# A mixture of experts on chosen rows in tiles of slots, after a routing stage of its own

## The reference

```
x  = x + L1_ffn(layernorm(x))
scores = softmax(xf @ Wg.T)                     # 8 experts
expert_weights, expert_indices = top_k(scores, 2)
gates  = one_hot(indices) * weights / sum(weights), summed over the two
h1, h3 = xf @ W1[e].T + low rank + b1[e],  xf @ W3[e].T + low rank + b3[e]     # 128 -> 256
y_e    = (silu(h1) * h3) @ W2[e].T + low rank + b2[e]                          # 256 -> 128
y      = sum over e of gates[e] * y_e
```

## Time and profile before

| what | us |
|---|---|
| median of 3 runs | 1125.36 (1123.95 to 1134.6) |
| the profiled execution | 1127.59 |
| its span, from the first to the last instruction | 1126.4 |
| mean granted TensorE clock | 0.834 of full speed |
| PE busy | 872.6 (77%) |
| DVE busy | 773.8 (69%) |
| ACT busy | 451.6 (40%) |
| POOL busy | 426.2 (38%) |
| moved by DMA | 37.98 MB |

### The profile page before, as it was taken

The page is one execution under the profiler, slowest core; times in us unless marked ns, Lnnn a source line. Parts: engine busy times, 40 slices in busy tenths (PEclk is TensorE's granted clock), DMA queues, the critical chain, the costliest instruction groups (busy, mean ns, idle before and its releaser), DMA issues. The chain is left out here.

```text
span 1126.4 us, 20278 instructions
## 1 busy us (share of the span) xinstructions
PE 872.6 (77%) x6496; PEld 644.1 (57%) x6496; DVE 773.8 (69%) x3299; ACT 451.6 (40%) x1123; POOL 426.2 (38%) x767
## 2 busy tenths in 40 slices
PE   0976766765577998537891388988699999999998
PEld 0753433432374554424561256666488888888887
DVE  7949999999334886371130869999567666766664
ACT  1454445444103555101132657877333333333332
POOL 5213666666545542016663655655200100010000
PEclk9975666667557999767996569999799999999999
DMA  8211111111103000005533100000000000000000
GB/s 171 64 40 31 36 36 35 37 36 31 30 13 150 19 23 24 10 6 100 84 107 121 45 2 3 3 3 3 1 1 10 11 1 11 10 10 1 10 10 10
DMA packets 66078, 37.98 MB, mean 34 GB/s; under 512 B 39482, under 2 KB 60083, under 8 KB 65460
## 3 DMA queue, kind: packets, MB, share of 16 engines
q1 hardware_dynamic: 63206, 32.31, 10.5%
q0 software_dynamic: 2048, 4.20, 2.5%
q10 hardware_dynamic: 718, 0.17, 0.1%
HBM read 26.11 MB, written 10.55 MB: 33 GB/s over the span
## 5 line engine op out<-in xcount | busy, mean ns | idle before, releaser
L1759 ACT ACTIVATE e_sg<-e_ps,vec 128x512 f32<-128x512 f32 x128 | 88.1, 689 | 182.7 <-PE e_ps L1720 182.0
L1680 PEld LDWEIGHTS e_psy<-w_folded,e_hh 128*128 128x128 f32 x1024 | 124.1, 192 | 5.2
L1680 PE MATMUL e_psy<-w_folded,e_hh 128*128 128x128 f32 x1024 | 124.5, 275 | 0.0
L1858 DVE SCALAR_TENSOR_TENSOR e_hh<-e_ps,vec,e_sg 128x512 f32<-128x512 f32 x128 | 94.6, 748 | 42.5 <-ACT e_sg L1759 39.7
L1846 DVE SCALAR_TENSOR_TENSOR X<-e_psy,e_gs,X 128x128 f32<-128x128 f32 x256 | 72.1, 344 | 56.5 <-PE e_psy L1680 56.5
L1718 PE MATMUL e_ps<-e_XH,e_wh 128*128 128x512 f32 x256 | 110.0, 430 | 0.0
L1720 PE MATMUL e_ps<-e_XH,e_wl 128*128 128x512 f32 x256 | 101.7, 397 | 0.0
L1719 PE MATMUL e_ps<-e_XL,e_wh 128*128 128x512 f32 x256 | 101.4, 396 | 0.0
L1448 POOL TENSOR_SCALAR a_kb<-a_kr,a_m,a_bk 128x128 f32<-128x128 f32 x128 | 57.9, 452 | 51.8 <-issue 36.8
L758 DVE MATCH_REPLACE8 work<-m,work 128x64 f32<-128x64 f32 x384 | 75.8, 208 | 0.0
L745 DVE MAX8 m<-work 128x8 f32<-128x64 f32 x384 | 57.1, 210 | 0.0
(11 more groups left out here) (367 smaller groups left out, 2135.8 us busy)
## 6 DMA issues: line engine op xcount, KB each, us to landing
toe<-s4d_kernel SPq DMA_DIRECT2D x64, 64.0 KB
planes<-rt_zeros SPq DMA_DIRECT2D x4, 1024.0 KB, 6.9
ew<-in_L_ffn_ew SPq DMA_DIRECT2D x16, 256.0 KB
comb_y<-planes SPq DMA_DIRECT2D x16, 256.0 KB, 5.7
X<-in_x SPq DMA_DIRECT2D x4, 512.0 KB, 6.8
fold_wr<-in_L_ffn_W SPq DMA_DIRECT2D x16, 128.0 KB, 2.3
rows<-XT SPq DMA_DIRECT2D x8, 256.0 KB, 2.0
out_dram<-X SPq DMA_DIRECT2D x8, 256.0 KB, 2.3
```

Of the source, the lines that this page charges most:

```text
L1680: mm = pe.matmul(psy[j][:, k, :], hh[j][:, c, k * P:(k + 1) * P], G.w2[:, e, c, :], start=(c == 0 and k == 0), stop=(c == NC - 1), skip_gr ...
L1759: act.activation(sg[j][:, c, :], psh[0][c][:], ACT.Silu, bias=G.vec[:, k:k + 1]).then_inc(silu[c], 1)
L1858: dve.scalar_tensor_tensor(hh[j][:, c, :], psh[1][c][:], G.vec[:, k:k + 1], sg[j][:, c, :], ALU.add, ALU.mult).then_inc(hh_sb[c], 1)
```

## The change

- `second_experts` is replaced by three stages: `second_router`, `second_experts`, `combine_pairs`.
- `second_router` goes through the 8 blocks: statistics, normalising, logits, the choice of two experts, gates, the rank of each row within its expert (a matmul against a triangle of ones plus running sums), and from it the row's slot in DRAM. GpSimd scatters each normalised row twice, once for each choice, with 8 indirect transfers of 128 rows in a block, each row with its home (where its result goes) and its gate (130 words, 520 bytes). The gated biases are added to `G.X` here. At the end VectorE makes a table: for each of 23 tiles (the most that 2 x 4096 rows can need in tiles of 512 slots with 8 experts) its expert and its first slot.
- `second_experts` does 23 tiles. SyncE reads expert and slot from the table into registers and loads the tile's rows (266 KB), its expert's split first-layer weights (4096 bytes a partition, 524 KB), and the second-layer weights with biases (1040 bytes a partition, 133 KB). The tile's results are scaled and scattered to DRAM with four indirect transfers. Unused slots hold zeros and a spare home.
- `combine_pairs` loads both results of each row, adds them to `G.X` and stores it.
- `first_experts` also writes the split and folded weights of all experts to DRAM. `second_attention` also writes empty rows to all 40448 slots: 79 stores of 266 KB.

The diff, cut (`NX, NW, NY = 4, 3, 3` are the buffers of rows, weights and results; `S` = 4):

```diff
+STILE = 512
+NTILE = 2 * B * T // STILE + NE - 1
+SROWS = (NE - 1) * B * T + NTILE * STILE
+SPARE = 2 * B * T
+ROW = D + 2
# first_experts, SyncE
+                kept = G.folded.rearrange("e p w -> p e w")
+                later += [(kept[:, :, n13:n13 + n2], G.w2[:].rearrange("p e c d -> p e (c d)"))]
...
+                sp.wait_ge(s["low"], NE)
+                for m, w in enumerate((G.wh, G.wl)):
+                    later += [(kept[:, :, 2 * HE * m:2 * HE * (m + 1)], w[:].rearrange("d e m c p -> d e (m c p)").bitcast(F32))]
+                    sp.dma_start(*later[-1]).then_inc(s["later"], 16)
# second_attention, SyncE
+                sp.wait_ge(s["vacant"], 1)
+                for i in range(n):
+                    sp.dma_start(slots[:, i, :, :], vacant[:]).then_inc(s["cleared"], 16)
+                sp.wait_ge(s["cleared"], n * 16)
# second_router, GpSimd
+                root(0)
+                root(1)
+                for b in range(NBLK):
+                    if b + 2 < NBLK:
+                        root(b + 2)
+                    pool.wait_ge(s["slot"], b + 1)
+                    pool.wait_ge(s["twice"], b + 1)
+                    for k in range(2):
+                        for t in range(TB):
+                            pool.indirect_dma_start(G.slots, bass.IndirectOffsetOnAxis(ap=slot[:, b, k, t:t + 1], axis=0),
+                                                    rb[b % NB][:, k, t, :], None).then_inc(sent[b % NB], 16)
# second_router, VectorE
+                for b in range(NBLK):
+                    if b + 2 < NBLK:
+                        statistics(b + 2)
+                    choose(b)
+                    if b + 1 < NBLK:
+                        normalise(b + 1)
+                    gates(b)
+                    place(b)
+                    if b > 0:
+                        add_biases(b - 1)
+                table()
# second_experts, SyncE
+                for i in range(NTILE):
+                    e = sp.value_load(G.tiles[0:1, 0, i:i + 1], min_val=0, max_val=NE - 1)
+                    row = sp.value_load(G.tiles[0:1, 1, i:i + 1], min_val=0, max_val=SROWS - STILE)
+                    if i >= NX:
+                        sp.wait_ge(kept[(i - NX) % NY], ((i - NX) // NY + 1) * S * 16)
+                    sp.dma_start(xr[i % NX][:], G.slots[bass.ds(row, STILE), :].rearrange("(p k) w -> p k w", k=S)).then_inc(rows[i % NX], 16)
+                    after(sp, s["y"], i - NW + 1)
+                    after(sp, hh_sb[NC - 1], i - NW + 1)
+                    split = wsp[i % NW][:].rearrange("d q m c p -> d (q m c p)").bitcast(F32)
+                    sp.dma_start(split, G.folded[bass.ds(e, 1), :, 0:WS].rearrange("a p w -> p (a w)")).then_inc(weights[i % NW], 16)
+                    sp.dma_start(wf[i % NW][:], G.folded[bass.ds(e, 1), :, WS:WS + WF].rearrange("a p w -> p (a w)")).then_inc(weights[i % NW], 16)
# second_experts, TensorE
+                def turn(i):
+                    pe.wait_ge(rows[i % NX], (i // NX + 1) * 16)
+                    after(pe, s["x_low"], i - 1)
...
                 turn(0)
+                for i in range(NTILE):
+                    j = i % 2
+                    if i + 1 < NTILE:
+                        turn(i + 1)
+                    pe.wait_ge(s["x_low"], i + 1)
+                    pe.wait_ge(weights[i % NW], (i // NW + 1) * 32)
+                    wh, wl = (wsp[i % NW][:, q, :, :, :] for q in range(2))
                     for c in range(NC):
                         for m in range(2):
...
+                    if i > 0:
+                        product(i - 1)
+                product(NTILE - 1)
# second_experts, GpSimd
+                for i in range(NTILE):
+                    pool.wait_ge(s["y_sb"], i + 1)
+                    for k in range(S):
+                        pool.indirect_dma_start(G.pair, bass.IndirectOffsetOnAxis(ap=home[i % NY][:, k:k + 1], axis=0),
+                                                ys[i % NY][:, k, :], None).then_inc(kept[i % NY], 16)
# second_experts, VectorE, in the order low(i + 1), the product of both halves of tile i, take(i - 1)
+                def take(i):
+                    dve.wait_ge(s["y"], i + 1)
+                    after(dve, kept[i % NY], i // NY * S * 16)
...
+                    for k in range(S):
+                        m = dve.tensor_scalar(ys[i % NY][:, k, :], psy[i % 2][:, k, :], xr[i % NX][:, k, D + 1:D + 2], None, ALU.mult)
+                    m.then_inc(s["y_sb"], 1)
# combine_pairs, SyncE: 16 loads of 256 KB, then a store of a block after each "both"; VectorE: two additions a block
```

More of the change, by code:

```diff
@@ new lines, in two @@
+            return [C.sb(f"r2_{name}{j}", shape, dt, ctx=ctx) for j in range(2)]
+        gs, bd, wg, wgt = (G.moe[n] for n in ("gs", "bd", "wg", "wgt"))
+        rb = [C.sb(f"r2_rows{j}", [P, 2, TB, ROW], ctx=ctx) for j in range(NB)]
+        xf = two("xf", [D, TB * P])
+        full = {n: C.sb("r2_" + n, [P, NT] + k, ctx=ctx) for n, k in (
+            ("st", [6]), ("mv", [2]), ("v", []), ("rstd", []), ("lg", [NE]), ("e", [NE]), ("idx", []), ("m0", []), ("m1", []), ("d", []),
+            ("q", []), ("sel", [NE]), ("pos", [NE]))}
@@ L1653, in tiles @@
+        sent = [C.sem(f"r2_sent{j}") for j in range(NB)]
         def tiles(b):
@@ new lines, in choose @@
+                    largest(b, 1)
+                    TT(w["d"], w["m1"], w["m0"], ALU.subtract).then_inc(s["d"], 1)
+                    step.then(TT(w["sel"], oh[:, b, 0, :, :], oh[:, b, 1, :, :], ALU.add))
+                    for t in range(b * TB, (b + 1) * TB):
+                        m = TT(run[:, t + 1, :], run[:, t, :], full["sel"][:, t, :], ALU.add)
+                        if t + 1 < (b + 1) * TB:
+                            step.then(m)
+                    m.then_inc(s["sel"], 1)
@@ new lines, in place @@
+                def place(b):
+                    w = part(b)
+                    dve.wait_ge(s["ranks"], b + 1)
+                    step.then(TT(w["pos"], psr[:, 0:TB * NE].rearrange("p (k e) -> p k e", e=NE), wide(first[:].unsqueeze(1), shape), ALU.add))
+                    step.then(TT(prod[:, b], oh[:, b], wide(w["pos"].unsqueeze(1), [P, 2, TB, NE]), ALU.mult))
+                    step.then(dve.tensor_reduce(slotf[:, b], prod[:, b], AX.X, ALU.add))
+                    dve.tensor_copy(slot[:, b], slotf[:, b]).then_inc(s["slot"], 1)
@@ new lines, in _ @@
+                statistics(0)
+                statistics(1)
+                dve.memset(run[:, 0, :], 0.0)
+                step.did(TS(first[:], G.iota8[:], float(B * T), float(NE * B * T), ALU.mult, ALU.add))
+                dve.wait_ge(s["iota"], 2)
+                step.then(dve.tensor_copy(tile_f[:], tile_i[:]))
+                normalise(0)
+                for b in range(NBLK):
[6 more added lines that the diff above has]
+                    place(b)
+                    if b > 0:
+                        add_biases(b - 1)
```

441 lines of the change are left out of this document (254 added, 187 removed).

## The result

The changed kernel takes 1161.91 us (median of 4 runs, 1157.49 to 1168.67) against 1125.09 before (median of 4): ratio 1.031, 95% interval 1.024 to 1.039. It is slower by 37 us, where 60 were forecast. The profiled execution took 1168.67 us, with a span of 1167.5.

A forecast was written before the change was run, and what follows sets the result against it. TensorE's work bound the old stage; the row buffers' loop would bind the new. Router 106 us, experts about 235, sum of pairs about 30 gave span 1186, 60 over 1126.4: 1185 us from 1125, range 1142 to 1255.

The forecast's parts named there:

- What bounds the kernel now: Old second experts: bound by TensorE's work, 4.55 us a place; 23 tiles for 64 places remove 187 us of it.
- Part 1: Router stage: GpSimd's scatters bind at 11.6 us a block with an inverse root, VectorE just behind; 106 us in all.
- Part 2: Changes of stage: 8.5 us from last scatter to next load; after the router 16.1 us to tile 0's matmuls.
- Part 3: Experts' tiles: the row buffers' loop through scaling, scatters, landing and load sets 21.0 us a pair, 10.5 a tile.
- Rival B: Experts' tiles: same loop with short landings and a clock that stays up, 8.5 us a tile, 1146 us; chance 0.17.
- Rival C: Experts' tiles: scaling, scatter, landing and load fit one slot, so PE binds at 5.1 us a tile; 1082 us; chance 0.09.
- Rival D: Router and experts: signals held up while GpSimd issues, 56 us and some 15 more; 1255 us; chance 0.14.
- Rival E: Scatters in router and experts: VectorE's shared port lock adds 0.29 us each, 19 and 11 us; 1215 us; chance 0.04.
- Part 4: Sum of pairs: 8.5 us to the first load, 13.3 of loads, then additions and stores; 28.6 us in all.
- Part 5: Edits elsewhere: emptying slots hidden under the attention; folded weights' late stores 0 to 8 us, taken 1; small steps 0.

The follow-up runs named there:

- group 2: Runs on one chip, kernel before at 1121.07 us: freed rows with half the scatters or three tiles' weights; changed kernel with sum in the experts' block or earlier weight stores.
- group 3: Runs on one chip, kernel before at 1120.85 us: rows freed at the scaling with four weight buffers, 1075.46 us, and the fastest version, 1066.27 us.
- kernel with few weights: Changed kernel with row buffers freed by the scaling and weights loaded for the first three tiles only: 1076.19 us.
- group 1: Runs on one chip, kernel before at 1128.06 us: rows freed at scaling 1128.12, six row buffers 1124.96, three tiles' weights 1174.85, one choice scattered in the router 1147.43.
- group 4: Runs on one chip, kernel before at 1126.95 us: freed rows, loaded ahead of weights, 1138.24 us; changed kernel with six row and four weight buffers, 1122.42 us.
- both kernels meant to test it: Changed kernel with row buffers freed by the scaling, plus half the experts' scatters (1071.63 us) or weights for three tiles only (1076.19 us).
- runs with half the scatters: Router scattering only each row's first choice, against the changed kernel, 1147.43 us; experts scattering two of four groups, with rows freed at the scaling, 1071.63 us.
- freed kernel: Changed kernel with row buffers freed once a tile is scaled, not once its scatters have landed: 1128.12 us with three weight buffers, 1075.46 with four.
- fastest version: Changed kernel with rows freed at scaling, five row buffers, sum in the experts' block, first-layer weights loaded unsplit and split per tile: 1066.27 us, ratio 0.952.

## Why the prediction was right, and where it was off

It named the right mechanism and the right sign; the range held. The size was off: 37 us more instead of 60, the experts' stage 33 us below its forecast and the rest some 15 above, so that the total stands nearer to the forecast than its parts. By its own steps, in the profiled execution:

| step | forecast us | measured us | off |
|---|---|---|---|
| opening and earlier stages, unchanged code | 0 | 7.8 | +7.8 |
| first experts, late stores | +1 | +5.1 | +4.1 |
| attention, emptying the slots | 0 | -0.4 | -0.4 |
| router, to the last issue's end | 106 | 103.9 | -2.1 |
| to the first matmul of tile 0 | 16.1 | 17.6 | +1.5 |
| experts, to the last issue's end | 235 | 201.8 | -33.2 |
| sum of pairs | 28.6 | 32.6 | +4.0 |

The sum of the last column is -18.3, and 1186 - 18 is the span of 1167.5.

- **What bounds the kernel now** and the work removed: right. TensorE's busy time fell by 177 us in the stage (315.0 to 137.5), 187 forecast for the places.
- **Part 1.** Right, and tested: GpSimd binds, block period 11.5 us ((884.24 - 826.51) / 5, the starts of the scatters in blocks with an inverse root ahead of them) against 11.6, VectorE behind it at 10.1.
- **Part 2.** Right within 1.5 us in the router's place.
- **Part 3**, the term that was mis-sized. The loop is there link by link and was the whole loss, but its links are shorter: scaling 1.9 (2.2), issues 4.75 (4.8), landing 1.45 (3.5, from 1053.30 to 1054.75), load 2.8 (3.3), together 10.9 instead of 13.8, and the slot that follows 6.3 (7.2; 1040.38 to 1046.68). That is 17.2 us in this pair instead of 21.0. Over the nine pairs the links take 10.5 and the slot 7.1, which is 17.6: the slot was right, and of the 3.3 us too many in the links the landing is 2. TensorE waits 4.0 to 5.8 us in a pair and not some 8. The landing stands below its lower bound of 2.0, and that bound was not like for like: the earlier trace rows count a store from its issue, the forecast a landing from the end of one. From its issue a scatter takes 0.96 + 1.45 = 2.4 us. The clock fell and rose as said: the first slot of the pair has 0.78 and transposes of 1.11 us for four, the next 5.1 us have 1.00 and transposes of 0.60. The estimate from the Trainium skill (DMA: Bandwidth & Descriptors, section "Anatomy of one DMA"), 9.5 us a tile, stood nearer to the 8.6 than mine. Its landing of 2.15 us, put behind the end of the issue, is above the row's 1.45, and counted from the issue it is below the 2.4; its 2.6 for the load applied a figure for transfers from GpSimd to one from SyncE, which took 2.8. One sum is half a microsecond too long: nine pairs of 21.0 us are 189.0 and not 189.5.
- **Rival B** (short landings and a clock that stays up, 8.5 a tile, 1146 us) has the tile's number by luck: the clock did not stay up (a first slot of 7.1 us on average and not 5.1), and the landing was shorter than its 2.0. The total lies above it by what went the other way, the opening, the stores and the sum.
- **Rival C's condition** was not met, but its price was right: with the loop gone a tile takes 5.2 to 5.3 us on the chips of groups 2 and 3 (TensorE turns one every 4.99 in the kernel with few weights).
- **Rival D.** It doesn't show in the changed kernel's experts, where the list has no remote wait. With the loop gone such waits do appear on the chips of groups 1 and 4, beside tiles of 6.65 to 7.0 us. That GpSimd's issuing holds the signals up, as D has it, no run shows: both kernels meant to test it ran on a chip without such waits. I had read the earlier trace rows as a property of the kernel; it goes with the chip on which that trace was taken.
- **Rival E.** Its price did not come: the router's scatters have a median of 958 ns, and the longest, 1110, is the first of all. The 3100 ns that the Trainium skill (SBUF — State Buffer, section "SBUF: two separate sides") gives for a transfer from GpSimd beside such a copy on VectorE stand in no trace here. A rare and small form of it is not excluded: the two longest indirect transfers on record, 1.49 us each, began 0.03 and 0.04 us after a subtraction on VectorE (572.59 and 975.59 us in the two traces of group 3).
- **Part 4.** 4 us short: the end of a stage costs 11.1 us after these scatters and not the 8.5 of the earlier trace rows. As the runs with half the scatters show (8.3 and 7.4), it depends on what GpSimd issued before.
- **Part 5.** The late stores cost 3.9 us (12.4 against the 8.5 of the earlier trace rows; 608.83 to 621.27), inside their 0 to 8 and not the 1 taken; the other 1 us in the table's row fell in the sum behind them. The emptying is hidden, as said.
- **The opening** is no part of the change: within group 1 the same unchanged code reached the first experts' first scatter at 526.7 us in one trace and at 535.1 in another. It moves one execution by 8 us; the median stands 7 below the profiled execution.

**What stays open.** What ends a wait marked remote, and why two of the groups' chips have it and two have none, was not found. The step from 6.8 to 5.2 us between the freed kernel with three weight buffers (group 1) and with four (group 3) is for the most part not the buffer's: with six row buffers, a fourth weight buffer took the stretch from 150.7 us (group 1) to 146.3 (group 4), 0.2 us a tile, on two chips that both have remote waits. That the rest is the chip's is likely and not shown, since no kernel of the experiments ran on both kinds of chip. So the fastest version's 4.8% holds for group 3's chip; on one with remote waits it was not run.

## What to carry to other kernels

When a tile's buffer is freed by the landing of its results though its last reader was long before, write the loop down: reader, issues, landing, load, and over how many slots it spans. Here that one wait was worth 34 to 39 us on a chip with remote waits, the whole loss of a change that saved 177 us of TensorE, and some 75 us on one without, where the freed kernel with four weight buffers is 4% faster than the kernel before (one run); freeing at the last read, or buffers enough that the loop spans more slots, both remove it. And compare kernels on one chip only, and look first at a stage that no edit touches: had I read the first experts' scatters of group 2 at once, two of my expectations would have been worded otherwise.

## What the hardware showed that I had not expected

- Chips differ in kind: from the first to the last scatter of the first experts eight traces, from groups 1 and 4 and of the two kernels compared, have 72 to 74 us and remote waits, six have 64.2 us and none. The kernel before takes 1128.06 and 1126.95 us on the first kind, 1121.07 and 1120.85 on the second.
- A scatter's landing in mid-stage is seen 1.45 us after its issue ends, but a stage that ends behind indirect transfers loses about 11 us to the next load (7.4 and 8.3 behind half the scatters), of which 9.8 vanish if the same engine's queue simply goes on within the stage.
- GpSimd issues an indirect transfer of 128 rows every 1.26 us, over 92 of them (115.0 us for 91 steps in the kernel with four weight buffers), with TensorE, VectorE and 235 GB/s of transfers beside it; at 5.05 us a tile it is then as near to binding as TensorE.
